# Preln attention and low-rank FFN on one core: scores ahead of the values' projection, P in the odd bank, all second products behind the output projection

## The chip, the cores and the metric

The kernel runs on one core of a Trainium2 chip. The metric is the device time of one execution in microseconds (us). PE is TensorE, DVE is VectorE, ACT is ScalarE, POOL is GpSimd, SP is the queue that issues most transfers.

## The reference

Input x has 4 batches of 2048 positions with 512 features. All is float32. Cut to what matters:

```
z  = layernorm(layernorm(x)) * ln_g + ln_b          # attention block
q, k, v = split(z @ W_qkv + b_qkv)                   # 16 heads of 32
gate = sigmoid(layernorm(x) @ W_gate + b_gate); gate /= mean(gate) + eps
q = relu(q * gate)**2 + eps ; k = relu(k * gate)**2 + eps
state_t = state_(t-1) + k_t v_t ;  sums_t = sums_(t-1) + k_t     # causal, per head
attn_t = (q_t . state_t) / (q_t . sums_t + eps)
x1 = x + attn @ W_proj + b_proj

P = layernorm(x1) @ U1          # 512 -> 128         # FFN block
H = gelu(P @ V1 + b1)           # 128 -> 2048
Q = H @ U2                      # 2048 -> 128
out = x1 + Q @ V2 + b2          # 128 -> 512
```

## The kernel before, in words

**Tiling.** The rows are cut into 64 chunks of 128 positions, taken round robin over the four batches. The program is unrolled: `steps` (L97) calls `step(p, b)` for p = 0 to 16 and b = 0 to 3 in each engine's block, and each engine runs its own list in order. In one step three chunks are in work: `n`, which is projected, `c`, one older, whose attention is finished, and `d`, two older, which enters the FFN. The FFN works on groups of two chunks (256 rows) spread over two steps: an odd step (b = 1, 3) computes P and the first four of eight "pairs" of the hidden layer, the even step after it the other four. A pair is 256 hidden features: `h_pair` (L831) is its first product (six matmuls of 256 columns), the gelu is on ACT (`gelu`, L471), the high part of the result on DVE (`h_head`, L618), the low part on POOL (`h_tail`, L392), and `q_pair` (L845) is its second product (six matmuls). Steps with n, c and the FFN together are the 61 from chunk 3 to chunk 63, 31 odd and 30 even. The steps before them load the weights, and four steps after them finish.

**Precision.** A product of float32 matrices is three matmuls of high and low parts (`product`, L789, lines 793 to 795), so each operand has a "hi" copy (ACT, or DVE for H) and a "lo" one.

**TensorE's order in one step (from L856).** GATE projection; transposes of the queries of c (tq); KEY projection; transposes of the normalized x1 of d (tx); in an odd step the result products; QUERY projection; transposes of the keys of c (tk); in an odd step P (L921), in an even one the first pair; VALUE projection (L930); the first pair in an odd step, and then the second pair; scores of c (L949, 32 matmuls of a 32-row tile); pairs three and four; the second product of the first pair; attention output (L968 with the state, 32x32 tiles, and L974 with the masked scores, 128x32 tiles); transposes of the next chunk (tz); the second product of the second pair; state products (L988, 128x32 tiles); running key sums (L998, L999); output projection y (L1006); second products of pairs three and four.

**Who gates them.** Scores overwrite the four banks that tk and QUERY wrote, so they wait for ACT's copy `key_t` (L501) and for DVE's first step of the queries (L608). DVE masks the scores into `probs` (L698) before the output products may run. The output products also overwrite the bank of VALUE, so they wait for `values` (L688). The output's own hi and lo copies (ACT L520, DVE L707) come before the key sums, which overwrite one of its banks. P lies in `ps_c`, a bank of the scores; the pairs alternate between the banks `ps_h[0]` and `ps_h[1]`. DVE's end of a step is the division chain from `key_sums` (L727) on, then x1 and its normalization (L773); on POOL follow the small statistics, the addition of the FFN bias (L404) and of the projection bias (L384). Near the start DVE also makes the low parts of three weight tiles (`tile_tails(early_tiles)`, L692).

```
if ffn.exists:
    h_pair(ffn, pairs[2])
    h_pair(ffn, pairs[3])
    q_pair(ffn, pairs[0])
if c.exists:
    ...
    pe.wait_ge(s["probs_ready"], c.done())
```

Of the kernel before, what the change touches and what calls it, by code (L numbers as in the profile page):

```python
# [23 lines left out]
F32 = mybir.dt.float32  # L24
F32R = mybir.dt.float32r
ALU = mybir.AluOpType
# [3 lines left out]
P = 128  # L30
# [73 lines left out]
def block_kernel(nc, x, ln_g, ln_b, w_qkv, b_qkv, w_gate, b_gate, w_proj, b_proj,  # L104
                 u1, v1, b1, u2, v2, b2, out, carry_dram):
    ctx = ExitStack()
    with ctx:
# [231 lines left out]
        def _(pool):  # L339
# [57 lines left out]
            def step(p, b):  # L397
# [8 lines left out]
                add_bias(n)  # L406
                if ffn.exists and b % 2 == 0 and not is_last(p):
                    h_tail(ffn, pairs[0])
                if n.exists:
# [3 lines left out]
                        .then_inc(s["key_ready"], 1)  # L413
                if ffn.exists and not is_last(p):
                    if b % 2:
                        h_tail(ffn, pairs[0])
                if n.exists:
                    pool.wait_ge(s["key_hi_ready"], n.done())
                    E.tensor_tensor(key_lo[:, :], keys[:, n.half, :], key_hi[:, :].bitcast(F32),
                                    ALU.subtract).then_inc(s["key_lo_ready"], 1)  # L420
                if ffn.exists and not is_last(p):
                    h_tail(ffn, pairs[1])
                    h_tail(ffn, pairs[2])
                    h_tail(ffn, pairs[3])
# [12 lines left out]
        def _(act):  # L437
# [42 lines left out]
            def step(p, b):  # L480
# [52 lines left out]
        def _(dve):  # L533
# [94 lines left out]
            def step(p, b):  # L628
# [42 lines left out]
                if n.exists:  # L671
# [4 lines left out]
                    squared_relu(n, s["query_done"], s["query_steps"], ps_b, QUERY, queries[:, :])  # L676
                x_norm(Chunk(p, b + 1))
                if b % 2 and ffn.exists:
                    dve.wait_ge(s["pt_hi_ready"], ffn.done())
                    E.tensor_tensor(pt_lo[:, :], ps_c[:, 0:GROUP], pt_hi[:, :].bitcast(F32), ALU.subtract)\  # L680
# [10 lines left out]
                if isinstance(p, int) and 4 * p + b == 0:  # L691
                    tile_tails(early_tiles)  # L692
                if ffn.exists and b % 2:
                    h_head(ffn, pairs[0], finishing)
                if c.exists:
                    dve.wait_ge(s["scores_done"], c.done())
                    blocks = HPG * KT
                    E.tensor_tensor(probs[:, :, :].rearrange("p j (k t) -> p (j k) t", k=KT),  # L698
                                    scores.rearrange("p (g t) -> p g t", g=blocks),
                                    causal.unsqueeze(1).broadcast_to([P, blocks, P]), ALU.mult)\  # L700
                        .then_inc(s["probs_ready"], 1)
                if ffn.exists:
                    h_head(ffn, pairs[1], finishing)
                    h_head(ffn, pairs[2], finishing)
                if c.exists:
                    dve.wait_ge(s["ot_hi_ready"], c.done())
                    E.tensor_tensor(ot_lo[:, :, :], out_cols, ot_hi[:, :, :].bitcast(F32), ALU.subtract)\  # L707
                        .then_inc(s["ot_ready"], 1)
                    dve.wait_ge(s["state_done"], c.done())
                    E.tensor_tensor(state_of(c, 1).rearrange(flat), state_cols(c), state_of(c).rearrange(flat),  # L710
                                    ALU.add).then_inc(s["state_ready"], 1)
                z_tail(Chunk(p, b + 1))
                if ffn.exists:
                    h_head(ffn, pairs[3], finishing)
                if n.exists:
# [70 lines left out]
        def _(pe):  # L786
# [69 lines left out]
            def step(p, b):  # L856
# [57 lines left out]
                if b % 2 and ffn.exists:  # L914
                    if isinstance(p, int) and p == 0:
                        pe.wait_ge(s["stage_lo"], len(tiles))

                    pe.wait_ge(s["x1t_ready"], d.done())
                    if result.exists:
                        pe.wait_ge(s["result_ready"], result.chunk(0).done())  # L920
                    product(ps_c[:, 0:GROUP], [(u1_hi[:, k, :], u1_lo[:, k, :]) for k in range(KT)],  # L921
                            [(x1t_hi[:, k, :], x1t_lo[:, k, :]) for k in range(KT)]).then_inc(s["p_done"], 1)
                if ffn.exists and b % 2 == 0:
                    h_pair(ffn, pairs[0])
                if n.exists:
                    if not c.exists:
                        bias_products(2)
                        pe.wait_ge(s["stage_lo"], FIRST)
                    pe.wait_ge(s["key_steps"], n.done(3, 1))
                    project(VALUE, ps_a, s["value_done"])  # L930
                if ffn.exists and b % 2:
                    h_pair(ffn, pairs[0])
                if ffn.exists:
                    h_pair(ffn, pairs[1])
                if c.exists:

                    if n.exists:
                        pe.wait_ge(s["query_steps"], n.done(3, 1))
                    else:
                        pe.wait_ge(s["den_steps"], c.done(6, 1))  # L940
                    pe.wait_ge(s["key_t_ready"], c.done())
                    if result is not None and result.exists:
# [9 lines left out]
                    mm.then_inc(s["scores_done"], 1)  # L952
                if ffn.exists:
# [3 lines left out]
                if c.exists:  # L957
                    if n.exists:
# [22 lines left out]
                if ffn.exists:  # L981
                    q_pair(ffn, pairs[1])
                if c.exists:
                    for ft in range(KT):
                        for j in range(HPG):
                            cols = slice(ft * P + HEAD * j, ft * P + HEAD * (j + 1))

                            mm = E.matmul(state_cols(c)[HEAD * j:HEAD * (j + 1), ft * HEAD:(ft + 1) * HEAD],  # L988
                                          keys[:, c.half, cols], values[:, c.half, cols],
                                          start=not ffn.exists and ft == 0, stop=True,  # L990
                                          tile_position=(0, HEAD * j), skip_group_check=True)
                    mm.then_inc(s["state_done"], 1)
                if n.exists:

                    if c.exists:
# [43 lines left out]
```

## Time and profile before

| | us |
|---|---|
| median of 3 runs | 1784.44 (1784.2 to 1786.72) |
| the profiled execution | 1784.35 |
| its span in the trace | 1782.3 |
| PE busy | 1740.6 (98%) |
| DVE busy | 1334.1 (75%) |
| POOL busy | 829.8 (47%) |
| ACT busy | 676.3 (38%) |

The profiled execution's time holds the span and 2.05 us around it. Starts in the trace are us from the span's start, the second column of a timeline is a duration in us. The end of a matmul is modelled and overlaps the next start, so the time of TensorE's work is read between starts.

### The profile page before, as it was taken

How to read it: one execution, taken by the hardware profiler on the slowest of the kernel's cores; microseconds unless marked ns; L12 is line 12 of the kernel's file. 1: busy time of each engine (PE TensorE's matmuls, PEld its weight loads, DVE VectorE, ACT ScalarE, POOL GpSimd, SP SyncE). 2: the span in 40 equal slices, each digit the busy share in tenths (PEclk: the TensorE clock that was granted, in tenths of full speed). 3: DMA queues.
4: the chain of work that ended last, by engine and by line, in shares of the span. 5: the costliest groups of instructions: out<-in, count | busy, mean ns of one | idle time of the engine just before them, and what ended most of it. 6: DMA issues, size and time to landing. Idle time of an engine off the chain costs nothing.

```text
span 1782.3 us, 39774 instructions
## 1 busy us (share of the span) xinstructions
PE 1740.6 (98%) x16729; PEld 1465.8 (82%) x16729; DVE 1334.1 (75%) x2222; ACT 676.3 (38%) x1242; POOL 829.8 (47%) x1027
## 2 busy tenths in 40 slices
PE   7899999999999999999999999999999999999997
PEld 4688888888888888888888888888888888888876
DVE  6877777777777777777777777777777777777765
ACT  4243333333434433433433433433333334334332
POOL 3354445444544544544544454445455445445440
PEclk9999999999999999999999999999999999999999
DMA  6101010011010011010010100110100110100000
GB/s 209 34 19 37 25 37 25 25 37 37 25 37 25 25 36 37 25 36 25 25 37 26 36 26 26 35 37 25 37 25 25 37 37 25 37 25 25 31 20 24
DMA packets 34720, 61.41 MB, mean 34 GB/s; under 512 B 3864, under 2 KB 6448, under 8 KB 34544
## 3 DMA queue, kind: packets, MB, share of 16 engines
q1 hardware_dynamic: 33680, 57.31, 10.0%
q8 instruction: 133, 2.18, 0.5%
q10 hardware_dynamic: 864, 1.57, 0.3%
q14 instruction: 43, 0.35, 0.1%
HBM read 41.96 MB, written 16.91 MB: 33 GB/s over the span
## 4 chain that ended last, share of the span: by engine, by line
PE 92%; DVE 2%; issue 1%; ACT 0%; POOL 0%
PE wide L793 18%; PE wide L795 18%; PE wide L794 18%; PE wide L800 7%; PE ps_h L793 4%; PE wide L949 4%; PE wide L974 3%; PE ps_q L793 3%; PE ps_h L794 3%; PE ps_q L794 3%; PE ps_h L795 3%; PE ps_q L795 3%; PE wide L968 2%; PE wide L998 1%; PE ps_q L988 1%; PE wide L999 1%
## 5 line engine op out<-in xcount | busy, mean ns | idle before, releaser
L394 POOL TENSOR_TENSOR h_lo<-h_full,h_hi 128x512 fp32r<-128x512 f32 x244 | 318.3, 1314 | 439.6 <-DVE h_hi L620 439.6
L793 PE MATMUL wide<-wx_hi,zt_hi 128*128 128x512 f32 x1024 | 415.3, 406 | 5.5 <-DVE key_sums L723 3.1
L795 PE MATMUL wide<-wx_hi,zt_lo 128*128 128x512 f32 x1024 | 405.7, 396 | 0.0
L794 PE MATMUL wide<-wx_lo,zt_hi 128*128 128x512 f32 x1024 | 405.0, 396 | 0.0
L475 ACT ACTIVATE h_full<-ps_h,cols 128x256 f32<-128x256 f32 x512 | 203.9, 474 | 127.9 <-PE ps_h L795 127.4
L795 PEld LDWEIGHTS wide<-wx_hi,zt_lo 128*128 128x128 f32 x1024 | 192.7, 188 | 46.7
L793 PEld LDWEIGHTS wide<-wx_hi,zt_hi 128*128 128x128 f32 x1024 | 193.4, 189 | 43.5 <-DVE zt_lo L575 5.8
L794 PEld LDWEIGHTS wide<-wx_lo,zt_hi 128*128 128x128 f32 x1024 | 193.4, 189 | 37.7 <-issue 0.7
L357 POOL TENSOR_TENSOR small<-moments,eps_col 128x1 f32<-128x1 f32 x128 | 25.7, 201 | 396.7 <-DVE moments L762 327.0
L698 DVE TENSOR_TENSOR probs<-wide,causal 128x2048 f32<-128x2048 f32 x64 | 146.6, 2291 | 49.6 <-PE wide L949 49.5
L486 ACT ACTIVATE query_t<-wide 128x512 f32<-128x512 f32 x64 | 38.3, 598 | 363.5 <-PE wide L800 363.5
L793 PE MATMUL ps_h<-pt_hi,v_hi 128*128 128x256 f32 x512 | 153.7, 300 | 1.4 <-DVE pt_lo L680 0.9
L793 PE MATMUL ps_q<-h_hi,u_hi 128*128 128x256 f32 x512 | 150.0, 293 | 0.7 <-POOL h_lo L394 0.2
L794 PE MATMUL ps_h<-pt_lo,v_hi 128*128 128x256 f32 x512 | 144.6, 282 | 0.0
L794 PE MATMUL ps_q<-h_lo,u_hi 128*128 128x256 f32 x512 | 144.2, 282 | 0.0
L795 PE MATMUL ps_h<-pt_hi,v_lo 128*128 128x256 f32 x512 | 143.7, 281 | 0.0
L795 PE MATMUL ps_q<-h_hi,u_lo 128*128 128x256 f32 x512 | 143.1, 280 | 0.0
L620 DVE CAST h_hi<-h_full 128x512 fp32r<-128x512 f32 x256 | 102.5, 421 | 33.7 <-ACT h_full L475 33.7
L707 DVE TENSOR_TENSOR ot_lo<-wide,ot_hi 128x512 fp32r<-128x512 f32 x64 | 44.3, 692 | 104.9 <-ACT ot_hi L520 104.9
L501 ACT ACTIVATE key_t<-wide 128x512 f32<-128x512 f32 x64 | 38.3, 599 | 212.0 <-PE wide L800 212.0
L357 POOL TENSOR_TENSOR small<-small,minus_half 128x1 f32<-128x1 f32 x192 | 108.2, 563 | 15.1
L384 POOL TENSOR_TENSOR xs<-xs,bias_proj 128x512 f32<-128x512 f32 x64 | 110.5, 1727 | 5.4 <-DMA bias_out<-L_ffn_b 5.4
(150 smaller groups left out, 3865.2 us busy)
## 6 DMA issues: line engine op xcount, KB each, us to landing
xs<-L_attn_x SPq DMA_DIRECT2D x64, 256.0 KB, 2.8
out<-x1s SPq DMA_DIRECT2D x64, 256.0 KB, 2.1
key_sums<-carry_rows SPq DMA_DIRECT2D x60, 256.0 KB, 3.2
x1s<-L_attn_W_gate SPq DMA_DIRECT2D x4, 256.0 KB, 4.1
x1s<-L_ffn_U SPq DMA_DIRECT2D x4, 256.0 KB, 3.1
carry_rows<-key_sums SPq DMA_DIRECT2D x64, 2.0 KB
probs<-L_attn_W_qkv SPq DMA_DIRECT2D x3, 256.0 KB, 6.1
bias<-L_attn_b_qkv ACTq DMA_DIRECT2D x3, 256.0 KB, 6.8
```

The source lines that it names most:

```text
L357: E.tensor_tensor(out_, a, b, op).then_inc(sem_, 1)
L384: E.tensor_tensor(xs[:, c.slot, :], xs[:, c.slot, :], bias_proj[:, :], ALU.add)\
L394: E.tensor_tensor(h_lo[:, i % SLOTS, :], h_full[:, i % SLOTS, :], h_hi[:, i % SLOTS, :].bitcast(F32), ALU.subtract).then_inc(s["h_lo_ready ...
L475: last = E.activation(h_full[:, i % SLOTS, a * GROUP:(a + 1) * GROUP], ps_h[i % 2][:, a * GROUP:(a + 1) * GROUP], ACT.Gelu_apprx_tanh, bia ...
L620: E.tensor_copy(h_hi[:, i % SLOTS, :], h_full[:, i % SLOTS, :]).then_inc(s["h_hi_ready"], 1)
L698: E.tensor_tensor(probs[:, :, :].rearrange("p j (k t) -> p (j k) t", k=KT), scores.rearrange("p (g t) -> p g t", g=blocks), causal.unsquee ...
L793: E.matmul(ps, wh, mh, start=start and i == 0, stop=False)
L794: E.matmul(ps, wh, ml, start=False, stop=False)
L795: mm = E.matmul(ps, wl, mh, start=False, stop=stop and i == last)
L800: mm = E.transpose(ps_t[:, k * P:(k + 1) * P], src[:, k * P:(k + 1) * P], ident[:, :])
L949: mm = E.matmul(ps_scores[j][:, ft * P:(ft + 1) * P], key_t[rows, ft, :], query_t[rows, ft, :], start=True, stop=True, tile_position=(HEAD ...
L974: mm = E.matmul(ps_out[j][ft * HEAD:(ft + 1) * HEAD, 0:P], values[:, c.half, h * HEAD:(h + 1) * HEAD], probs[:, j, ft * P:(ft + 1) * P], s ...
```

## The change

No operation is added or removed. It moves these within each step:

- TensorE: scores go ahead of the VALUE projection. The state products go ahead of the attention output. The first product of the second pair (odd steps) and of the third go behind the next chunk's transposes, that of the fourth behind the key sums. The four second products all go behind the output projection. P is written to `ps_h[1]` and waits for the gelus of the group before; scores no longer wait for `pt_ready`.
- DVE: the masks come right after the queries (and P's low part), ahead of the values; the next chunk's `x_norm` behind the values and the early weight tiles; the state's sum and the first `h_head` ahead of `ot_lo`; the others behind `z_tail`.
- ACT: `key_hi` earlier, the gelus of later pairs behind `z_head`.
- POOL: all four `h_tail` behind `key_lo`.

```diff
@@ POOL
-                if ffn.exists and b % 2 == 0 and not is_last(p):
-                    h_tail(ffn, pairs[0])
...
-                if ffn.exists and not is_last(p):
-                    if b % 2:
-                        h_tail(ffn, pairs[0])
...
                 if ffn.exists and not is_last(p):
+                    h_tail(ffn, pairs[0])
                     h_tail(ffn, pairs[1])
@@ ACT
-                    E.activation(pt_hi[:, :], ps_c[:, 0:GROUP], ACT.Copy).then_inc(s["pt_hi_ready"], 1)
+                    E.activation(pt_hi[:, :], ps_h[1][:, 0:GROUP], ACT.Copy).then_inc(s["pt_hi_ready"], 1)
                 if ffn.exists and b % 2 == 0:
                     gelu(ffn, pairs[0])
-                if ffn.exists and b % 2:
-                    gelu(ffn, pairs[0])
-                if ffn.exists:
-                    gelu(ffn, pairs[1])
                 if n.exists:
                     act.wait_ge(s["key_ready"], n.done())
...
                 if ffn.exists:
-                    gelu(ffn, pairs[2])
-                    gelu(ffn, pairs[3])
+                    gelu(ffn, pairs[0 if b % 2 else 1])
                 if c.exists:
                     act.wait_ge(s["ot_done"], c.done())
...
                 z_head(Chunk(p, b + 1))
                 if ffn.exists:
+                    if b % 2:
+                        gelu(ffn, pairs[1])
+                    gelu(ffn, pairs[2])
+                    gelu(ffn, pairs[3])
@@ DVE
-                x_norm(Chunk(p, b + 1))
                 if b % 2 and ffn.exists:
                     dve.wait_ge(s["pt_hi_ready"], ffn.done())
...
-                if ffn.exists and b % 2 == 0:
-                    h_head(ffn, pairs[0], finishing)
+                if c.exists:
+                    dve.wait_ge(s["scores_done"], c.done())
+                    (probs, as below, moved here)
                 if n.exists:
                     (values)
...
                     tile_tails(early_tiles)
-                if ffn.exists and b % 2:
+                x_norm(Chunk(p, b + 1))
+                if c.exists:
+                    dve.wait_ge(s["state_done"], c.done())
+                    (state sum, moved here)
+                if ffn.exists:
                     h_head(ffn, pairs[0], finishing)
                 if c.exists:
-                    dve.wait_ge(s["scores_done"], c.done())
-                    (probs)
+                    dve.wait_ge(s["ot_hi_ready"], c.done())
+                    (ot_lo, moved here)
+                z_tail(Chunk(p, b + 1))
                 if ffn.exists:
                     h_head(ffn, pairs[1], finishing)
                     h_head(ffn, pairs[2], finishing)
-                if c.exists:
-                    (ot_lo, state sum)
-                z_tail(Chunk(p, b + 1))
-                if ffn.exists:
                     h_head(ffn, pairs[3], finishing)
@@ TensorE
-                    if result.exists:
-                        pe.wait_ge(s["result_ready"], result.chunk(0).done())
-                    product(ps_c[:, 0:GROUP], ...
+                    wait(pe, s["h_full_ready"], Group(ffn.p, ffn.off - 1).done(PAIRS, PAIRS))
+                    product(ps_h[1][:, 0:GROUP], ...
...
-                if n.exists:
-                    (VALUE projection)
-                if ffn.exists and b % 2:
-                    h_pair(ffn, pairs[0])
-                if ffn.exists:
-                    h_pair(ffn, pairs[1])
                 if c.exists:
...
-                    if b % 2 and ffn.exists:
-                        pe.wait_ge(s["pt_ready"], ffn.done())
                     (scores)
+                if n.exists:
+                    (VALUE projection, moved here)
                 if ffn.exists:
-                    h_pair(ffn, pairs[2])
-                    h_pair(ffn, pairs[3])
-                    q_pair(ffn, pairs[0])
-                if c.exists:
+                    h_pair(ffn, pairs[0 if b % 2 else 1])
+                if c.exists:
+                    pe.wait_ge(s["value_ready"], c.done())
+                    (state products, moved here; start=ft == 0 and (b % 2 == 1 or not ffn.exists))
                     (attention output)
                 tz(Chunk(p, b + 1))
                 if ffn.exists:
-                    q_pair(ffn, pairs[1])
-                if c.exists:
-                    (state products)
+                    if b % 2:
+                        h_pair(ffn, pairs[1])
+                    h_pair(ffn, pairs[2])
                 if n.exists:
                     (key sums)
+                if ffn.exists:
+                    h_pair(ffn, pairs[3])
                 if c.exists:
                     (output projection)
                 if ffn.exists:
                     if c.exists:
                         pe.wait_ge(s["state_ready"], c.done())
-                    q_pair(ffn, pairs[2])
-                    q_pair(ffn, pairs[3])
+                    for i in pairs:
+                        q_pair(ffn, i)
```

In this cut a name in parentheses stands for the block of that name.

## Rows read from the trace of the kernel before

**Rows 1.** The page, busy us of each engine

```profile
PE 1740.6 (98%) x16729; PEld 1465.8 (82%) x16729; DVE 1334.1 (75%) x2222; ACT 676.3 (38%) x1242; POOL 829.8 (47%) x1027
```

**Rows 2.** Groups by line and form, PE: busy us, mean ns, idle us before

```profile
L968 PE MATMUL wide<-query_t,state 32*32 32x128 f32 x1920 | 30.8, 278 | 8.1
```

**Rows 3.** Timeline, PE, an even step that ends at 843.07: start, us

```profile
827.91 0.39 PE L793 MATMUL wide<-wx_hi,zt_hi 128*128 128x512 f32 x1
...
831.51 1.17 PE L949 MATMUL wide<-query_t,key_t 32*128 32x128 f32 x32
...
834.72 0.28 PE L795 MATMUL ps_q<-h_hi,u_lo 128*128 128x256 f32 x1
835.14 0.51 PE L968 MATMUL wide<-query_t,state 32*32 32x128 f32 x32
835.58 1.08 PE L974 MATMUL wide<-probs,values 128*32 128x128 f32 x32
836.60 0.66 PE L800 MATMUL wide<-ident,zs 128*128 128x128 f32 x4
...
837.68 0.28 PE L795 MATMUL ps_q<-h_hi,u_lo 128*128 128x256 f32 x1
837.89 0.46 PE L988 MATMUL ps_q<-values,keys 128*32 128x32 f32 x32
838.28 0.50 PE L998 MATMUL wide<-key_hi,causal 128*128 128x512 f32 x1
838.62 0.40 PE L999 MATMUL wide<-key_lo,causal 128*128 128x512 f32 x1
...
842.95 0.28 PE L795 MATMUL ps_q<-h_hi,u_lo 128*128 128x256 f32 x1
843.07 0.39 PE L793 MATMUL wide<-wx_hi,zt_hi 128*128 128x512 f32 x1
```

**Rows 4.** Timeline, DVE, the same step

```profile
824.78 1.09 DVE L611 SCALAR_TENSOR_TENSOR keys<-keys,gate_scale,gate 128x512 f32<-128x512 f32 x1
...
826.39 1.18 DVE L615 SCALAR_TENSOR_TENSOR keys<-keys 128x512 f32<-128x512 f32 x1
827.50 0.74 DVE L608 SCALAR_TENSOR_TENSOR queries<-wide,small,bias 128x512 f32<-128x512 f32 x1
...
830.91 0.75 DVE L688 SCALAR_TENSOR_TENSOR values<-wide,small,bias 128x512 f32<-128x512 f32 x1 [0.29 <-PE wide L795]
832.75 2.29 DVE L698 TENSOR_TENSOR probs<-wide,causal 128x2048 f32<-128x2048 f32 x1 [1.09 <-PE wide L949]
...
837.36 0.69 DVE L707 TENSOR_TENSOR ot_lo<-wide,ot_hi 128x512 fp32r<-128x512 f32 x1 [1.65 <-ACT ot_hi L520]
...
839.57 0.68 DVE L727 TENSOR_TENSOR key_sums<-wide,key_sums 128x512 f32<-128x512 f32 x1
```

**Rows 5.** Timeline, ACT, the same step

```profile
827.40 0.60 ACT L501 ACTIVATE key_t<-wide 128x512 f32<-128x512 f32 x1 [2.63 <-PE wide L800]
```

**Rows 6.** Timeline, POOL, the same step

```profile
824.02 1.30 POOL L404 TENSOR_TENSOR x1s<-x1s,bias_out 128x512 f32<-128x512 f32 x1
825.27 1.75 POOL L384 TENSOR_TENSOR xs<-xs,bias_proj 128x512 f32<-128x512 f32 x1
```

**Rows 7.** Timeline, PE, the steps before the FFN begins

```profile
38.90 0.47 PE L793 MATMUL wide<-wx_hi,zt_hi 128*128 128x512 f32 x1 [3.10 <-DVE key_sums L723]
...
56.71 1.93 PE L974 MATMUL wide<-probs,values 128*32 128x128 f32 x32 [2.79 <-DVE probs L698]
...
82.29 1.08 PE L974 MATMUL wide<-probs,values 128*32 128x128 f32 x32 [2.80 <-DVE probs L698]
```

**Rows 8.** Timeline, DVE, the end of the first step

```profile
37.47 0.68 DVE L575 TENSOR_TENSOR zt_lo<-wide,zt_hi 128x512 fp32r<-128x512 f32 x1
```

**Rows 9.** Timeline, PE, the first step without a chunk to project

```profile
1743.23 1.17 PE L949 MATMUL wide<-query_t,key_t 32*128 32x128 f32 x32
...
1746.87 0.51 PE L968 MATMUL wide<-query_t,state 32*32 32x128 f32 x32
```

More of the change, by code:

```diff
@@ L676, in step @@
                     squared_relu(n, s["query_done"], s["query_steps"], ps_b, QUERY, queries[:, :])
-                x_norm(Chunk(p, b + 1))
                 if b % 2 and ffn.exists:
                     dve.wait_ge(s["pt_hi_ready"], ffn.done())
-                    E.tensor_tensor(pt_lo[:, :], ps_c[:, 0:GROUP], pt_hi[:, :].bitcast(F32), ALU.subtract)\
+                    E.tensor_tensor(pt_lo[:, :], ps_h[1][:, 0:GROUP], pt_hi[:, :].bitcast(F32), ALU.subtract)\
                         .then_inc(s["pt_ready"], 1)
-                if ffn.exists and b % 2 == 0:
-                    h_head(ffn, pairs[0], finishing)
+                if c.exists:
+                    dve.wait_ge(s["scores_done"], c.done())
+                    blocks = HPG * KT
+                    E.tensor_tensor(probs[:, :, :].rearrange("p j (k t) -> p (j k) t", k=KT),
+                                    scores.rearrange("p (g t) -> p g t", g=blocks),
+                                    causal.unsqueeze(1).broadcast_to([P, blocks, P]), ALU.mult)\
+                        .then_inc(s["probs_ready"], 1)
                 if n.exists:
@@ L692, in step @@
                     tile_tails(early_tiles)
-                if ffn.exists and b % 2:
-                    h_head(ffn, pairs[0], finishing)
-                if c.exists:
-                    dve.wait_ge(s["scores_done"], c.done())
[L697 to L701, printed above, removed]
-                if ffn.exists:
-                    h_head(ffn, pairs[1], finishing)
-                    h_head(ffn, pairs[2], finishing)
+                x_norm(Chunk(p, b + 1))
+                if c.exists:
+                    dve.wait_ge(s["state_done"], c.done())
+                    E.tensor_tensor(state_of(c, 1).rearrange(flat), state_cols(c), state_of(c).rearrange(flat),
+                                    ALU.add).then_inc(s["state_ready"], 1)
+                if ffn.exists:
+                    h_head(ffn, pairs[0], finishing)
                 if c.exists:
@@ L708, in step @@
                         .then_inc(s["ot_ready"], 1)
-                    dve.wait_ge(s["state_done"], c.done())
-                    E.tensor_tensor(state_of(c, 1).rearrange(flat), state_cols(c), state_of(c).rearrange(flat),
-                                    ALU.add).then_inc(s["state_ready"], 1)
                 z_tail(Chunk(p, b + 1))
                 if ffn.exists:
+                    h_head(ffn, pairs[1], finishing)
+                    h_head(ffn, pairs[2], finishing)
                     h_head(ffn, pairs[3], finishing)
@@ L918, in step @@
                     pe.wait_ge(s["x1t_ready"], d.done())
-                    if result.exists:
-                        pe.wait_ge(s["result_ready"], result.chunk(0).done())
-                    product(ps_c[:, 0:GROUP], [(u1_hi[:, k, :], u1_lo[:, k, :]) for k in range(KT)],
+                    wait(pe, s["h_full_ready"], Group(ffn.p, ffn.off - 1).done(PAIRS, PAIRS))
+                    product(ps_h[1][:, 0:GROUP], [(u1_hi[:, k, :], u1_lo[:, k, :]) for k in range(KT)],
                             [(x1t_hi[:, k, :], x1t_lo[:, k, :]) for k in range(KT)]).then_inc(s["p_done"], 1)
@@ L924, in step @@
                     h_pair(ffn, pairs[0])
-                if n.exists:
[L926 to L930, printed above, removed]
-                if ffn.exists and b % 2:
-                    h_pair(ffn, pairs[0])
-                if ffn.exists:
-                    h_pair(ffn, pairs[1])
                 if c.exists:
@@ L952, in step @@
                     mm.then_inc(s["scores_done"], 1)
+                if n.exists:
+                    if not c.exists:
+                        bias_products(2)
+                        pe.wait_ge(s["stage_lo"], FIRST)
+                    pe.wait_ge(s["key_steps"], n.done(3, 1))
+                    project(VALUE, ps_a, s["value_done"])
                 if ffn.exists:
-                    h_pair(ffn, pairs[2])
-                    h_pair(ffn, pairs[3])
-                    q_pair(ffn, pairs[0])
+                    h_pair(ffn, pairs[0 if b % 2 else 1])
                 if c.exists:
+                    pe.wait_ge(s["value_ready"], c.done())
+                    for ft in range(KT):
+                        for j in range(HPG):
+                            cols = slice(ft * P + HEAD * j, ft * P + HEAD * (j + 1))
+                            mm = E.matmul(state_cols(c)[HEAD * j:HEAD * (j + 1), ft * HEAD:(ft + 1) * HEAD],
+                                          keys[:, c.half, cols], values[:, c.half, cols],
+                                          start=ft == 0 and (b % 2 == 1 or not ffn.exists), stop=True,
+                                          tile_position=(0, HEAD * j), skip_group_check=True)
+                    mm.then_inc(s["state_done"], 1)
                     if n.exists:
@@ L981, in step @@
                 if ffn.exists:
-                    q_pair(ffn, pairs[1])
-                if c.exists:
[L984 to L992, printed above, removed]
+                    if b % 2:
+                        h_pair(ffn, pairs[1])
+                    h_pair(ffn, pairs[2])
                 if n.exists:
```

## The prediction

> **What bounds the kernel now.** I read the page's busy shares first: TensorE is busy 1740.6 of 1782.3 us [rows 1], so time saved elsewhere is worth nothing unless TensorE starts something earlier. The change adds and removes no matmul. It can only gain in two kinds of gap between TensorE's starts: waits, and switches between kinds of matmul. So next I read TensorE's timeline of one even step [rows 3], start to start, because modelled ends overlap. Within a run of 256-column matmuls a start follows the last by 0.12 (842.95 to 843.07). From 838.62 to 842.95 lie one key-sum matmul, twelve of the output projection and twelve second products: (4.33 - 11 x 0.12) / 13 = 0.23 for a 512-column one. A pair of six is thus 0.71, a projection of twelve 2.80.
>
> Gaps, from the last start of one kind to the first of the next: second product to state products 0.21 (837.68 to 837.89); second product to output products 0.42 (834.72 to 835.14). The rest is a wait, although the profile names no releaser: `probs` starts at 832.75 and takes 2.29, to 835.04 [rows 4], and the output starts 0.10 behind it. The wait is 0.21. It is not peculiar to this step: 1920 matmuls of L968 are 60 blocks, with 8.1 us idle before them [rows 2], 0.135 each from a modelled end of 0.28, which is a start-to-start gap of 0.415. So DVE's mask ends last before the output in every step.
>
> **The sum, term by term,** against the profiled execution (1784.35; the median 1784.44 is the same within 0.1). A change of 0.2%, 3.6 us, is about what a measurement tells from none.
>
> 1. *The mask's wait goes.* Scores now come before VALUE, so between the scores' end and the output lie 2.80 (VALUE), 0.1 (first matmul behind the small ones), 0.71 (a pair) and the state products, over 4 us, against the mask's 2.29. Gain 0.21 in each of 61 steps.
>
> 2. *Fewer switches.* Before, a step has two blocks of small matmuls behind the scores: [L968, L974, tz] and [L988]. The second costs 0.21 to enter, 0.39 - 0.13 = 0.26 of its own, 0.13 from its last start to the key sums (32 starts, last one 0.46 - 0.20 after the first, the 0.20 being its modelled length; 838.28), and 0.34 instead of 0.23 for the first 512-column matmul behind it. After, L988 leads the first block: entry 0.21 stays, once; between L988 and L968 there is a new gap; the key sums follow a pair with no gap. Saved are 0.21 + 0.11 + 0.13 less 0.12 (the ordinary step from a pair to the sums) less the new gap: 0.33 less the gap. No row shows L988 to L968. Bounds: 0.01 (no switch at all, as inside either block) and 0.20 (L968's last start, 835.38, to L974, 835.58). I take 0.13, that behind L988 to the key sums, since the block that is left is the same one. Saved 0.20 a step, bounds 0.13 to 0.32. The Trainium skill (TensorEngine Tiling (Array Packing), Key Properties) says that changing the tiling mode drains the array: by it the five switches behind the scores become four, and the gap inside the block can't be nothing. The rows agree at 0.20 for 32x32 to 128x32. Were the order inside a block free, terms 1 and 2 would be 0.53 a step rather than 0.41.
>
> 3. *Even steps: key sums wait for `ot_lo`.* The output's low part starts 0.76 behind tz (837.36 less 836.60) and takes 0.69; with 0.07 for the signal (835.04 to the weight load ahead of 835.14) the sums can start 1.50 to 1.52 behind tz. Before, a second product and L988 lay between: 1.68 (836.60 to 838.28), so it was hidden with 0.16 to spare. Now an even step has tz and one pair there: 837.68 - 836.60 + 0.12 = 1.20. The wait is 0.30, and the first matmul behind it loses its early weight load, 0.34 instead of 0.23: 0.40 lost in 30 steps. An odd step has two pairs there, 1.91: nothing lost.
>
> 4. *Even steps: scores wait.* They may start at 827.91 + 0.09 = 828.00 now. ACT's `key_t` ends at 827.40 + 0.60 = 828.00 [rows 5], 0.07 for the signal: at least 0.07. DVE's first query step ends at 828.24 [rows 4]: 0.31. Between them POOL decides. L611 and L615 are short by themselves, but stood against POOL's additions here: L611 began at 824.78 inside L404 (824.02 to 825.27 [rows 6]) and ended 0.60 behind it; L384 then took 1.75; L615 began at 826.39 inside L384 and ended 0.55 behind it. DVE reaches L615 earlier or later with where these two lie, and they follow the division chain. That chain now starts behind the last pair's cast: the pair ends 5.6 us before the next step (2.80 and four second products of 0.71), and gelu and cast take some 1.4, so 4.2 before the step, against 843.07 - 839.57 = 3.5. With the additions 0.7 to 0.9 earlier, L384 runs into L611 (about 0.9 lost in place of 0.5) and L615 runs free: the query step ends about 828.14, a wait of 0.2. Bounds 0.07 to 0.35. In odd steps P (1.4) covers both.
>
> 5. *Other waits, costed at nothing.* `values` must be ready for L968: 0.20 + 0.75 + 0.07 = 1.02 behind VALUE (830.91 is 0.20 behind VALUE's end at 830.71), against 0.71 + 0.21 + 0.26 + 0.13, less 0.12, = 1.2: 0.2 to spare, if DVE is free. P's bank has been free since the gelu before the last projection. Second products come 3 us or more behind their pairs' first products, and POOL needs 1.3 a pair: about 0.4 to spare for the last. pt_lo has VALUE and scores to hide behind. The fourth pair in an odd step waits for the gelu of the second, about even: 0 to 0.1. SP's stores and the carried sums follow the division chain, which is earlier.
>
> 6. *Start.* In the first step `x_norm` moves behind three weight tiles, to where zt_lo starts now, 37.47 [rows 8]; transposes, zt_hi and zt_lo follow it, so zt_lo starts about 1.87 later, and GATE, waiting at 38.90 [rows 7], with it. In the two steps with a chunk to finish but no FFN, TensorE waits 2.79 and 2.80 for the mask (56.71, 82.29). VALUE now covers it and `values` ends last, 1.0 earlier; in the first of them the output also ran slow behind the wait (1.93 for 1.08), 0.85 more. Net +1.9 - 1.85 - 1.0 = -1.0.
>
> 7. *End.* One such mask wait without VALUE: scores at 1743.23 come a pair (0.71) earlier; 1.24 (831.51 to 832.75), 2.29 and 0.10 later the output starts at 1746.15 instead of 1746.87 [rows 9]: -0.7.
>
> Odd: 31 x -0.41 = -12.7. Even: 30 x (-0.41 + 0.40 + 0.20) = +5.7. Start and end -1.7. Sum -8.7: **1775.7**. With each unknown at its bounds: low end 61 x 0.12 + 30 x 0.13 = 11 further down (1764.5), high end 61 x 0.07 + 30 x 0.15 + 31 x 0.1 = 12 up (1787.6). Its own range is 1771 to 1781.
>
> **Rivals.**
>
> *The two halves cancel.* The gap inside the block costs 0.20 and the even scores wait 0.35: terms become 31 x -0.34 + 30 x 0.41 - 1.7 = about 0: 1784. For it: the L968 to L974 gap; the additions may fall just so that L611 stands through all of L384. Against it: L988's own exit is 0.13. Chance 0.22.
>
> *The order inside a block is free and `key_t` alone holds the scores:* 11 less than forecast, 1765. For it: tz (128x128) to the next product shows no such gap. Against: L968 to L974. Chance 0.12.
>
> *Slower: the casts lose to POOL.* Pairs two to four now come together, so DVE's casts meet POOL's `h_tail` (1.3 each), which they never did. Should the last cast stand behind a whole tail, the division chain starts at or behind its old place, the additions begin later than 824.02, L615 stands behind a later L384, and the query step ends 0.3 later still: scores wait 0.67 in 30 even steps, 0.47 more than forecast: +14, 1789.8. It decides from the point where L404 begins over 6.5 us into an even step. The Trainium skill (SBUF — State Buffer, Who interferes with whom) has DVE and GpSimd take one port pair in turn, whoever comes first, for a whole instruction; L611 and L615 in rows 4 and 6 agree. By that rule either cast could block. For the forecast: behind L404 it was DVE that got its turn, before POOL's next. Chance 0.14.
>
> *Nothing moves,* because all of it was hidden anyway: excluded for the mask by the 60 blocks; I give it the rest with small mixtures near the forecast.
>
> **Chances.** Forecast 0.50; with the fast rival and a share of the mixtures faster by over 0.2% is 0.61. The cancelling rival and its neighbours are within 0.2%: 0.24. Slower 0.15. To hold 8 in 10 the range leaves out part of the fast rival and of the slower one: 1766 to 1788.
>
> **What would show it.** Right: L968's idle of 8.1 gone; an even step about 0.2 longer than now, an odd one 0.41 shorter; L998 in even steps 1.50 behind tz with `ot_lo` as releaser, 30 times; scores in even steps released by ACT or DVE. Term 2 is read between L988's last start and L968. Wrong: output products released by `values`; L615 still 1.18 with L384 at its old place in the step; second products waiting for `h_lo`.

## The result, and the profile after

The changed kernel takes 1791.06 us (median of 10 runs, 1787.38 to 1791.88) against 1784.72 for the kernel before (10 runs): a ratio of 1.0028, 95% interval 1.0018 to 1.0037. It is 6.3 us or 0.28% slower (the interval's lower end, 0.18%, lies just under the 0.2% that the forecast called a change), outside the stated range of 1766 to 1788, and the forecast of 1775.7 was on the other side of the kernel before. The ten runs are not one heap: three lie at 1787.4 to 1787.6, one at 1789.65 and six at 1790.9 to 1791.9. The profiled execution, 1791.6, is one of the six, and its start shows it (below).

The profiled execution of the changed kernel has a span of 1789.5 us, 7.2 more than before. Its lines are numbered anew: L606 is the step of keys and queries that was L611, L610 the one that was L615, L603 was L608, L633 `x1t_lo` was L638, L929 the scores, L947 the state products, L962 and L968 the output, L984 and L985 the key sums, L786 to L788 `product`, L793 the transposes that were L800. In experiments that add lines, the same instructions stand up to four lines further down. The page's busy shares, which answer to [rows 1]:

```profile
PE 1743.9 (97%) x16729; PEld 1460.4 (82%) x16729; DVE 1407.3 (79%) x2222; ACT 680.4 (38%) x1242; POOL 834.0 (47%) x1027
```

TensorE's matmuls are the same. DVE is 73 us busier with the same 2222 instructions: a first sign of instructions that stand against something. The waits of the changed kernel (who waited for whom: us in total, times, longest), those of the weight load PEld, where a wait shows in full:

```profile
PEld wide L793 <- DVE x1t_lo L633: 22.9, 31, 1.7
PEld wide L984 <- DVE ot_lo L701: 12.8, 32, 1.1
...
PEld wide L929 <- DVE queries L603: 9.3, 32, 1.0
...
PEld ps_h L786 <- ACT h_full L471: 6.7, 32, 0.4
```

Three of the four were forecast: key sums for `ot_lo`, scores for the queries or `key_t`, and the odd fourth pair for the gelu of the second. The first and largest was not: the transposes of the keys (tk) wait for `x1t_lo` 31 times, in 28 of the 30 even steps for 0.66 or 0.67 each, and three times near the start and the end. (The time in this view is that of the weight load; between TensorE's starts less of it is lost.) TensorE's timeline of an even step of the changed kernel:

```profile
825.85 0.60 PE L793 MATMUL wide<-ident,queries 128*128 128x128 f32 x4
...
832.08 0.40 PE L788 MATMUL wide<-wx_hi,zt_lo 128*128 128x512 f32 x1
832.70 0.66 PE L793 MATMUL wide<-ident,keys 128*128 128x128 f32 x4 [0.22 <-DVE x1t_lo L633]
833.11 0.36 PE L786 MATMUL ps_h<-pt_hi,v_hi 128*128 128x256 f32 x1
...
833.79 0.28 PE L788 MATMUL ps_h<-pt_hi,v_lo 128*128 128x256 f32 x1
834.14 1.17 PE L929 MATMUL wide<-query_t,key_t 32*128 32x128 f32 x32
835.24 0.50 PE L786 MATMUL wide<-wx_hi,zt_hi 128*128 128x512 f32 x1
...
838.72 0.28 PE L788 MATMUL ps_h<-pt_hi,v_lo 128*128 128x256 f32 x1
838.93 0.46 PE L947 MATMUL ps_q<-values,keys 128*32 128x32 f32 x32
839.32 0.53 PE L962 MATMUL wide<-query_t,state 32*32 32x128 f32 x32
839.77 1.08 PE L968 MATMUL wide<-probs,values 128*32 128x128 f32 x32
840.78 0.66 PE L793 MATMUL wide<-ident,zs 128*128 128x128 f32 x4
...
841.87 0.28 PE L788 MATMUL ps_h<-pt_hi,v_lo 128*128 128x256 f32 x1
842.30 0.50 PE L984 MATMUL wide<-key_hi,causal 128*128 128x512 f32 x1
...
852.02 0.60 PE L793 MATMUL wide<-ident,queries 128*128 128x128 f32 x4
```

From tq to tq the step takes 26.17, against 25.57 before. Read downward: tk starts at 832.70, not at 832.31 (832.08 + 0.23), and takes 0.06 longer with its load behind the wait: 0.45 lost. Scores start 0.35 behind the last h matmul, not 0.21: 0.14 lost. The output (839.32) follows the state products with no wait for the mask: the old 0.21 is gone. The key sums start at 842.30 instead of 841.99 and lose 0.10 more in the load: 0.41. What ended late in DVE's and POOL's timelines:

```profile
829.54 0.75 DVE L603 SCALAR_TENSOR_TENSOR keys<-wide,small,bias 128x512 f32<-128x512 f32 x1
830.32 1.72 DVE L606 SCALAR_TENSOR_TENSOR keys<-keys,gate_scale,gate 128x512 f32<-128x512 f32 x1
831.97 0.68 DVE L633 TENSOR_TENSOR x1t_lo<-wide,x1t_hi 128x512 fp32r<-128x512 f32 x1
832.57 0.68 DVE L610 SCALAR_TENSOR_TENSOR keys<-keys 128x512 f32<-128x512 f32 x1
```

```profile
828.96 1.29 POOL L404 TENSOR_TENSOR x1s<-x1s,bias_out 128x512 f32<-128x512 f32 x1
830.21 1.28 POOL L384 TENSOR_TENSOR xs<-xs,bias_proj 128x512 f32<-128x512 f32 x1
```

POOL's addition L384 starts at 830.21, 0.11 ahead of L606 at 830.32. L606 stands through the whole addition (to 831.49) and ends 0.55 behind it, at 832.04: 1.72 instead of the 1.09 of [rows 4]. `x1t_lo` ends at 832.65 and tk's load follows at once. In [rows 4, 6] the same two engines met, but L404 ran first and L384 was still behind it, so that DVE had its turn between the two.

The start, in PE's timeline of the changed kernel's profiled execution, answers to [rows 7]:

```profile
36.30 0.39 PE L788 MATMUL wide<-wx_hi,zt_lo 128*128 128x512 f32 x1
39.87 1.12 PE L793 MATMUL wide<-ident,zs 128*128 128x128 f32 x4 [3.17 <-DVE zs L554]
...
43.09 0.76 PE L786 MATMUL wide<-wx_hi,zt_hi 128*128 128x512 f32 x1 [1.25 <-DVE key_sums L716]
...
79.85 2.09 PE L929 MATMUL wide<-query_t,key_t 32*128 32x128 f32 x32 [0.78 <-ACT key_t L497]
```

Before, the transposes followed VALUE directly. Now they wait 3.17 for `x_norm`, then GATE waits 1.25. All twelve GATE matmuls run 0.43 apart, 5.25 in all; before, some of the twelve ran at 0.23 to 0.31 and they took 4.42. Later the scores of the third step are slow too (2.09 for 1.17). From the last VALUE matmul to the keys' transposes of the next step, 36.3 to 54.7, the granted clock is 0.72; before, the same stretch, 34.7 to 49.4, had 0.88. (The columns are the stretch and its length, the busy time of PE, PEld, DVE, ACT and POOL, the granted clock, the DMA share and GB/s.)

```profile
36.30:54.70 18.40, 13.98 (x49) 10.47 (x48) 14.30 (x26) 5.03 (x10) 4.97 (x8) 0.72 0.44 130
```

```profile
34.70:49.40 14.70, 11.60 (x47) 8.91 (x46) 13.26 (x25) 5.36 (x10) 4.81 (x7) 0.88 0.55 162
```

That is a mixture of the two levels, 2.4 and 1.2 GHz, behind the idle time. By the third tq the changed kernel is 4.1 behind (95.02 against 90.96), of which 1.8 are from before VALUE's end (36.53 against 34.73): a gate weight that came 1 us later, and a first GATE projection and bias products behind it that took 0.8 longer, at the lower clock.

How much of the 4.1 belongs to the change, this one execution does not say. e5 (below) has the same first steps, instruction for instruction, and its profiled execution has the third tq at 89.85, 5.2 earlier than here and 1.1 earlier than before. Its GATE waits the same 1.25, its third scores the same 0.78, and they run at full speed:

```profile
76.16 1.17 PE L929 MATMUL wide<-query_t,key_t 32*128 32x128 f32 x32 [0.78 <-ACT key_t L497]
```

The tally of the spans by tq: start +4.1, the 61 intervals up to the last tq +5.1 (the 31 odd ones -11.7, the 30 even ones +16.8), the rest -2.0: +7.2. The steady part and the end alone are thus +3.1.

### The profile page after: what moved, and what is told of

The parts are those of the page before. It is cut to its first block, busy times and chain, and to the rows that moved or that the text cites. A ratio compares the mean times of both kernels' runs of the same rounds, so it can differ in the third digit from the quotient of the medians.

```text
span 1789.5 us, 39714 instructions
## 1 busy us (share of the span) xinstructions
PE 1743.9 (97%) x16729; PEld 1460.4 (82%) x16729; DVE 1407.3 (79%) x2222; ACT 680.4 (38%) x1242; POOL 834.0 (47%) x1027
## 3 DMA queue, kind: packets, MB, share of 16 engines
q10 hardware_dynamic: 864, 1.57, 0.3%
## 4 chain that ended last, share of the span: by engine, by line
PE 80%; DVE 8%; ACT 5%; issue 1%; POOL 0%
PE wide L786 14%; PE wide L787 14%; PE wide L788 14%; PE wide L793 5%; PE wide L929 4%; PE ps_h L786 4%; PE ps_h L787 4%; PE ps_h L788 4%; PE wide L968 4%; PE ps_q L786 3%; PE ps_q L788 3%; PE ps_q L787 3%; DVE keys L606 3%; ACT L486 2%; PE wide L962 2%; PE ps_q L947 1%
## 5 line engine op out<-in xcount | busy, mean ns | idle before, releaser
L394 POOL TENSOR_TENSOR h_lo<-h_full,h_hi 128x512 fp32r<-128x512 f32 x244 | 333.0, 1374 | 318.8 <-DVE h_hi L615 318.8
L786 PE MATMUL wide<-wx_hi,zt_hi 128*128 128x512 f32 x1024 | 422.8, 413 | 4.6 <-DVE zt_lo L570 3.0
L788 PE MATMUL wide<-wx_hi,zt_lo 128*128 128x512 f32 x1024 | 406.3, 397 | 0.0
L471 ACT ACTIVATE h_full<-ps_h,cols 128x256 f32<-128x256 f32 x512 | 211.2, 473 | 201.4 <-PE ps_h L788 194.2
L786 PEld LDWEIGHTS wide<-wx_hi,zt_hi 128*128 128x128 f32 x1024 | 193.8, 189 | 50.6 <-DVE zt_lo L570 5.3
L788 PEld LDWEIGHTS wide<-wx_hi,zt_lo 128*128 128x128 f32 x1024 | 193.2, 189 | 47.4
L615 DVE CAST h_hi<-h_full 128x512 fp32r<-128x512 f32 x256 | 165.2, 665 | 60.0 <-ACT h_full L471 60.0
L786 PE MATMUL ps_h<-pt_hi,v_hi 128*128 128x256 f32 x512 | 153.0, 299 | 1.4 <-DVE pt_lo L674 0.9
L414 POOL TENSOR_TENSOR key_lo<-keys,key_hi 128x512 fp32r<-128x512 f32 x64 | 83.4, 1304 | 139.3 <-ACT key_hi L506 139.3
L786 PE MATMUL ps_q<-h_hi,u_hi 128*128 128x256 f32 x512 | 144.7, 283 | 0.3
L788 PE MATMUL ps_h<-pt_hi,v_lo 128*128 128x256 f32 x512 | 144.0, 281 | 0.0
L788 PE MATMUL ps_q<-h_hi,u_lo 128*128 128x256 f32 x512 | 143.8, 281 | 0.0
```

The source lines that it names most:

```text
L394: E.tensor_tensor(h_lo[:, i % SLOTS, :], h_full[:, i % SLOTS, :], h_hi[:, i % SLOTS, :].bitcast(F32), ALU.subtract).then_inc(s["h_lo_ready ...
L471: last = E.activation(h_full[:, i % SLOTS, a * GROUP:(a + 1) * GROUP], ps_h[i % 2][:, a * GROUP:(a + 1) * GROUP], ACT.Gelu_apprx_tanh, bia ...
L615: E.tensor_copy(h_hi[:, i % SLOTS, :], h_full[:, i % SLOTS, :]).then_inc(s["h_hi_ready"], 1)
L786: E.matmul(ps, wh, mh, start=start and i == 0, stop=False)
L788: mm = E.matmul(ps, wl, mh, start=False, stop=stop and i == last)
```

## The experiments

Theory A: L384 takes its turn just ahead of L606, and tk waits for what stands behind. Rival B: DVE is late as a whole, because its casts now meet POOL's low parts (mean cast 665 ns against 421), and the place of the addition is of no matter. All times below are medians, with the ratio to runs of the kernel before that were taken beside them (medians 1784.24 to 1784.75). Step lengths are from tq to tq in the profile.

| kernel | us | ratio, 95% | even | odd |
|---|---|---|---|---|
| before | 1784.7 | | 25.57 | 28.40 |
| changed | 1791.06 | 1.0028 (1.0018 to 1.0037) | 26.18 | 28.05 |
| e1 | 1774.21 | 0.9938 (0.9925 to 0.9952) | 25.74 | 28.05 |
| e2 | 1776.1 | 0.9952 (0.9939 to 0.9964) | 25.76 | 28.05 |
| e3 | 1759.37 | 0.9857 (0.9843 to 0.9870) | 25.32 | 28.05 |
| e4 | 1840.35 | 1.0312 (1.0298 to 1.0326) | 26.55 | 29.27 |
| e5 | 1778.61 | 0.9960 (0.9948 to 0.9973) | 25.77 | 28.05 |
| e6 | 1791.16 | 1.0033 (1.0022 to 1.0044) | 25.85 | 28.41 |
| e7 | 1854.47 | 1.0393 (1.0379 to 1.0408) | 27.17 | 29.19 |
| e8 | 1784.72 | 1.0003 (0.9994 to 1.0012) | 26.18 | 28.06 |
| e9 | 1787.47 | 1.0016 (1.0007 to 1.0025) | 25.65 | 28.39 |

**e1: the addition elsewhere.** Changed kernel, POOL:

```diff
-                add_bias(n)
...
                     E.tensor_tensor(key_lo[:, :], keys[:, n.half, :], key_hi[:, :].bitcast(F32),
                                     ALU.subtract).then_inc(s["key_lo_ready"], 1)
+                add_bias(n)
```

> The changed kernel with POOL's addition of the projection bias (L384) moved behind key_lo. Theory A (the addition takes the shared port 0.1 us before DVE's L606 starts, so L606 takes 1.72, x1t_lo behind it ends late and the transposes of the keys wait): L606 of the keys falls to 0.75 or at most 1.3 in even steps, the transposes' wait for x1t_lo (0.45 with its lost weight load) is gone, scores wait at most 0.07: 30 even steps x 0.5 = 15 us less, 1776. Rival B (DVE is late as a whole, because its casts stand behind POOL's low parts, 665 against 421 ns; where the addition lies does not matter): L606 may shorten, the time stays within 2 us of 1791.

16.9 us less. In the groups of e1 (busy, mean ns) and its DVE and PE timelines of an even step:

```profile
L615 DVE CAST h_hi<-h_full 128x512 fp32r<-128x512 f32 x256 | 165.1, 664 | 60.1 <-ACT h_full L471 60.1
```

```profile
820.12 0.75 DVE L606 SCALAR_TENSOR_TENSOR keys<-keys,gate_scale,gate 128x512 f32<-128x512 f32 x1
820.78 0.68 DVE L633 TENSOR_TENSOR x1t_lo<-wide,x1t_hi 128x512 fp32r<-128x512 f32 x1
```

```profile
822.11 0.60 PE L793 MATMUL wide<-ident,keys 128*128 128x128 f32 x4
...
823.49 1.17 PE L929 MATMUL wide<-query_t,key_t 32*128 32x128 f32 x32
```

L606 is back at 0.75 and tk is released by nothing. The casts still take 664 ns, so they are not what held TensorE: rival B falls. The even step gets 0.44 shorter, which is the 0.45 read above. Between the third tq and the last, the profile of e1 is 12.5 shorter than that of the changed kernel; the other 4.9 of the spans lie ahead of the third tq, where the edit gives about 1.0 (tk at 78.41 waited 1.23, here 0.26) and the rest differs between executions, as e5 showed. Scores still start 1.38 behind tk, 0.14 too late: that is `key_t`, not DVE.

**e2: a wait added.** Ahead of `add_bias(n)`, `pool.wait_ge(s["key_steps"], n.done(3, 2))`.

> The changed kernel with one wait more: POOL starts the addition L384 only when L606 of the keys is done. Theory A: a wait added makes the kernel faster. L606 at 0.75, no wait for x1t_lo, but the addition now stands against L610, so the queries' first step is late and scores in even steps wait 0.3: net -0.28 x 30 = -8 us, 1783. Rival B: nothing gained, 1791 or more.

One wait more made the kernel 15 us faster, so it is the order in which the two engines come, not the amount of work. The addition now meets L612 (as L610 is there), but the queries' step that follows costs TensorE only 0.02 a step more than in e1. The 0.3 expected there was too much.

```profile
820.74 0.68 DVE L635 TENSOR_TENSOR x1t_lo<-wide,x1t_hi 128x512 fp32r<-128x512 f32 x1
821.34 1.40 DVE L612 SCALAR_TENSOR_TENSOR keys<-keys 128x512 f32<-128x512 f32 x1
822.66 0.74 DVE L605 SCALAR_TENSOR_TENSOR queries<-wide,small,bias 128x512 f32<-128x512 f32 x1
```

**e5: the fourth pair first.** Changed kernel, TensorE, even steps:

```diff
                     h_pair(ffn, pairs[2])
+                    if b % 2 == 0:
+                        h_pair(ffn, pairs[3])
                 (key sums)
-                if ffn.exists:
+                if ffn.exists and b % 2:
                     h_pair(ffn, pairs[3])
```

> The changed kernel with one edit: in even steps the fourth pair's first product goes ahead of the key sums. Theory A: the wait for ot_lo (0.30) and the late weight load behind it (0.10) go, 30 x 0.41 = 12 us less, 1779, and the wait for x1t_lo stays. If the last pair's earlier cast and low part move DVE's division chain earlier by more than 0.5, L384 could leave the place where it meets L606, and then up to 13 us more go (1766). Rival C (the key sums' wait only passes on to the output projection or to the second products): within 2 us of 1791.

12.5 us less (12.7 from lowest run to lowest run), even steps 0.41 shorter, tk's wait as it was. The wait for `ot_lo` was worth its whole length, and did not pass on.

**e8: the first step.** `x_norm(Chunk(0, 1))` again ahead of `add_rows(2)`.

> The changed kernel with the first step's x_norm back ahead of the early weight tiles, nothing else. Theory: the transposes of the second chunk follow the values' projection at once again, TensorE waits 3.1 once instead of 3.2 and 1.3, and the GATE projection behind them does not run wholly at the lower clock (12 matmuls in 4.4 rather than 5.3 us): 2.4 + 0.9 = 3.3 us less, 1787.7, steps after the third as in the changed kernel (26.19 and 28.05). Rival: the start waits for weights, so that nothing or under 1 us comes of it, 1790.5.

6.3 us less, and steady steps as in the changed kernel. PE's timeline has GATE waiting once again, as in [rows 7], and the scores at full speed:

```profile
38.43 0.47 PE L790 MATMUL wide<-wx_hi,zt_hi 128*128 128x512 f32 x1 [3.10 <-DVE key_sums L720]
...
73.90 1.17 PE L933 MATMUL wide<-query_t,key_t 32*128 32x128 f32 x32 [0.78 <-ACT key_t L497]
```

Twice what was expected, but the runs again fall into groups: nine of e8's eleven lie at 1784.3 to 1785.9 and two at 1787.5 and 1787.7, where the changed kernel had three of ten at 1787.4 to 1787.6 and six at 1790.9 to 1791.9. Lowest against lowest, the edit gives 3.05, near the 3.3 expected. The rest of the 6.3 is that more runs fell into the lower group. Whether the edit makes that likelier or the draw was lucky was not separated; the kernel before, too, has runs from 1783.4 to 1787.8.

**e3: three places mended,** the edits of e1, e5 and e8 together.

> The changed kernel with three places mended: the addition behind key_lo as in the run before, in even steps the fourth pair's first product ahead of the key sums (so 1.9 us instead of 1.2 lie between the transposes and the sums), and in the first step x_norm ahead of the early weight tiles as before the change. Theory A: -15, then the wait for ot_lo with its lost weight load goes, -0.41 x 30 = -12, and the first step gives back 2 to 3: 1762. Steps about 25.1 (even) and 28.0 (odd). Rival B: -14 only, 1777.

1759.37, 31.7 below the changed kernel and 25.3 (1.4%) below the one before. Step lengths 25.32 and 28.05 against 25.1 and 28.0. The three edits one by one gave 16.9, 12.5 and 6.3, or 35.7, 4 more than together; lowest run against lowest they gave 14.5, 12.7 and 3.1, or 30.2, and 28.6 together. So the medians of the single edits hold some of the scatter of the start.

**e6: the state products back,** on e3, as a block of their own ahead of the key sums (and DVE's sum behind `z_tail`).

> The run with three mended places (1759.4), with the state products put back behind the first products and ahead of the key sums, as a block of small matmuls of their own. This prices the switches alone, since no wait is near. The forecast's term: 0.21 to enter, 0.13 from its last start to the sums, 0.11 for the late load there, less the 0.12 and the 0.13 saved: 0.20 in each of 61 steps, +12, 1771.6. If every change of tile form drained alike (0.20 each), +0.13 a step, 1767.3; if the order inside a block were free, +0.32 a step, 1779.

It cost 31.8, not 12. Another wait had come in; waits of e6, and its PE timeline of an odd step:

```profile
PEld wide L956 <- DVE values L690: 20.0, 59, 0.3
PEld wide L797 <- DVE x1t_lo L633: 13.4, 33, 1.8
```

```profile
861.57 0.28 PE L792 MATMUL ps_h<-pt_hi,v_lo 128*128 128x256 f32 x1
861.98 0.51 PE L956 MATMUL wide<-query_t,state 32*32 32x128 f32 x32
...
865.25 0.28 PE L792 MATMUL ps_h<-pt_hi,v_lo 128*128 128x256 f32 x1
865.45 0.46 PE L981 MATMUL ps_q<-values,keys 128*32 128x32 f32 x32
865.84 0.50 PE L991 MATMUL wide<-key_hi,causal 128*128 128x512 f32 x1
```

The output starts 0.41 behind the pair, 0.20 more than a switch, since `values` is not there: the state products had covered it. The block itself shows 0.20 to enter and 0.13 to leave, as the forecast had it. So the lead of the state products pays twice, once in switches and once as cover. The odd steps grew by 0.36, the even ones by 0.54: the second row above is the reason for the difference. In 28 even steps tk waits for `x1t_lo` again, about 0.30 in the load, because DVE comes to L606 beside the other addition, L404, and L606 takes 1.35 to 1.37. e6 is therefore no clean price of the switches.

**e4 and e9: controls on the kernel before.** e4 moves `add_bias(n)` behind `key_lo` there, e9 behind the last `h_tail`.

> Control: the kernel before with the same addition moved behind key_lo. Theory A: nothing waits for L611 or x1t_lo there (no such row among TensorE's waits in steady state), so L611 and L615 get shorter and the time stays: 1784.7 within 1 us. Rival B': the addition weighs on DVE in any order, and this one gains too, 5 us or more.

> The control of before again, mended: in the run with the addition behind key_lo the addition stood in POOL's queue ahead of the FFN's low parts and second products waited for them 61 times. Now it goes behind the last low part of the step. Theory A: in the order before nothing waits for L611, L615 or x1t_lo, so L611 and L615 get shorter and the time stays, 1784.7 within 1.5 us. Rival: it gains 5 us or more also there.

e4 was badly placed: the addition stands in POOL's queue ahead of the low parts, and second products wait. Waits of e4:

```profile
PE ps_q L793 <- POOL h_lo L394: 42.1, 61, 1.2
```

It shows how little slack the order before had on POOL: one addition of 1.3 us, placed there, costs 55.6. In e9 nothing is gained and 2.7 to 3.2 are lost, 0.08 of it in each even step. But e9 is not the control that it was meant to be. L615 got shorter (0.68), L611 did not: in even steps it takes 1.35 where it took 1.09, since L404 now starts 3.97 behind tq instead of 3.72 and L611 stands behind it. So `x1t_lo` is late, and tk, which waited for it in two even steps of the kernel before, waits in all 30, 0.28 or more in the load. A wait and a DVE row of e9:

```profile
PEld wide L800 <- DVE x1t_lo L638: 12.7, 33, 1.7
```

```profile
826.89 1.35 DVE L611 SCALAR_TENSOR_TENSOR keys<-keys,gate_scale,gate 128x512 f32<-128x512 f32 x1
```

What a shorter L611 is worth in the old order stays open. What e9 does show is theory A's path once more: 0.26 more in L611 is enough to use up the slack of tk.

**e7: the mask alone.** The kernel before with scores ahead of VALUE, the masks beside it and P in the odd bank, the rest as before.

> The kernel before with the first part of the change alone: scores ahead of the values' projection, masks beside it, P in the odd bank; state products, FFN pairs, second products and POOL's order stay. Theory: the mask's wait goes, 61 x 0.21 = 13 us less, and the start and end give 3; DVE's division chain keeps its place, so no wait for x1t_lo; scores in even steps wait for DVE's first query step, 0.3 x 30 = +9. Sum 1778. Rival: the scores' wait is larger or the output then waits for the values; 1784 or more.

70 us slower, 76 off. Waits of e7:

```profile
PEld ps_q L793 <- POOL h_lo L394: 41.9, 63, 1.5
PEld ps_h L793 <- ACT h_full L475: 27.0, 64, 0.4
PEld wide L936 <- DVE queries L608: 15.0, 32, 1.0
```

With the scores gone from between them, four first products (three in an even step) and a second product stand in a row, and the waits are for gelu and low part, which can't follow. The two parts of the change belong together: the scores may go ahead only if the second products leave that place. That behind the output projection is the place for them was not tried apart from the rest.

## Why the prediction was wrong

**Terms 1 to 3 held.** The mask's wait went in the steady steps. The gap from L947's last start (838.93 + 0.26 = 839.19) to L962 is 0.13, the value taken between 0.01 and 0.20. The Trainium skill (TensorEngine Tiling (Array Packing), Key Properties) has a change of tiling mode drain the array; the rows show a gap at each change, yet not of one size: 0.13 behind the state matmuls (32 columns) and 0.20 behind the output's 32x32 ones (128 columns). The key sums lost 0.41, forecast 0.40, and e5 gives it back.

**Term 4 is the step that failed.** It foresaw that with POOL's additions earlier "L384 runs into L611 (about 0.9 lost in place of 0.5)". That happened: 0.97 lost, 1.72 for the 0.75 that it takes alone, against 1.09 before. But the term followed the delay only to the queries' step and the scores, and put 0.20 on them. Between L611 and L615 stands `x1t_lo`, and tk waits for it. That wait was not looked at: 0.45 a step, and the scores 0.14 on top, so 0.59 where 0.20 stood, 28 x 0.39 = 11 us. The trace of before had the numbers, in DVE's and PE's timelines of the step of [rows 3, 4]:

```profile
825.79 0.68 DVE L638 TENSOR_TENSOR x1t_lo<-wide,x1t_hi 128x512 fp32r<-128x512 f32 x1
```

```profile
826.77 0.60 PE L800 MATMUL wide<-ident,keys 128*128 128x128 f32 x4
```

`x1t_lo` ended 0.30 ahead of tk's start (826.47 against 826.77), less than the delay that was foreseen. That L384 and not L606 comes first hangs on 0.11 us. The Trainium skill (SBUF — State Buffer, Who interferes with whom) says that a DVE instruction with two SBUF inputs, as L606 is, contends with a GpSimd one that reads SBUF, and that the order of issue decides who blocks; e1 and e2 agree, where the same two instructions in the other order leave L606 at 0.75.

**Term 5** was right on `values` (nothing waits for it in steady state) and on the second products. The fourth pair's 0 to 0.1 was costed at nothing: the odd steps gained 0.35, not 0.41, which is 2 us, and this wait is at most that 0.06.

**Term 6** priced the start at -1.0; the changed kernel's profile has it at +4.1, that of e5, with the same first steps, at -1.1. So the term as a whole may be right for such an execution, and it is not shown to have failed. Its part of +1.9 for the later `x_norm` was too small: e8's edit gives 3.05 back from lowest run to lowest. It left out that GATE behind the second wait runs slowly, 5.25 here and 4.96 in e5 for 4.42 before.

**Term 7** held: from the last tq to the output lie 11.88 before and 11.24 after (-0.64, forecast -0.7). Another 1.4 came behind it, which the sum did not have: transposes at the end waited 1.79 for the normalized x1 before and 0.38 after.

**The sum.** Of the 15.9 us between the forecast's -8.7 and the spans' +7.2, 12 are in the steady steps, 11 of them term 4, 5 are in the start of this execution, and the end gives 1 back.

**The slower rival** had the sign and not the mechanism. It has L404 later and L615 standing behind L384; in truth both additions came earlier (L404 starts 3.1 behind tq, against 3.7 before), and L611 was hit. The casts did get longer, and no wait of TensorE in the steady steps of e1 goes back to them.

With the one wait gone (e1) the change is 10.5 us faster than before, near the forecast of 8.7, and not by luck in the steady steps: there e1 is 7.3 shorter than before, where terms 1 to 5 sum to 7.0.

## What to carry to other kernels

When a reorder moves one engine's work in time, write down for each pair of instructions on DVE and POOL that both read SBUF which comes first, and follow every instruction queued behind the one that loses, not the last of them only. Note beside each how long before its use it ends: a slack of 0.30 was lost here three times, in the changed kernel, in e6 and in e9, each time to an addition on POOL. A change that comes out slower may be three gains and one collision: undo nothing before the waits of the new trace are read, since here three small edits, one of them to the first step, turned +0.28% into -1.4%. Near a full engine, cover is shared: the mask alone lost 70 us, and the state products also covered the values.

## What was not expected of the hardware

One POOL addition of 1.3 us that starts 0.11 ahead of a DVE instruction costs it 0.97 (1.72 for 0.75). In the other order the addition pays: in [rows 4, 6] L384 came up while L611 was still at work, and it was L384 that grew, to 1.75, while L611, which had stood behind L404, ended 0.55 behind that one. Casts from SBUF to SBUF get longer as well when they run beside POOL's low parts (0.42 in the median, up to 1.57; before the change at most 0.45). TensorE's clock fell once more near the start of the changed kernel's profiled execution, behind idle times of 1.23 and 0.78 us: the granted clock from 79 to 83 was 0.58, a mixture of the levels 2.4 and 1.2 GHz, and the scores took 2.09 for 1.17. Behind the same two idle times e5 was granted 1.00 and took 1.17, so these do not decide alone. No step of the steady part shows such scores; the end does, at 2.09 in e1.
